# Feed-forward part of layer 0 woven into the attention loop, its gated value made by two products of VectorE from PSUM

## What is computed

```
x = x + tanh(g_xattn[0]) * causal attention(layernorm(x), ctx)        16 heads of 8
x = x + tanh(g_ffn[0])   * down(silu(gate(q(n))) * up(q(n)))          n = layernorm(x)
x = x + tanh(g_xattn[1]) * attention(layernorm(x), 8 chosen keys per head)
x = x + tanh(g_ffn[1])   * mixture of 16 experts, two chosen, and a shared one
```

## Time and profile before

| | us |
|---|---|
| median of 3 runs | 180.67 (180.66 to 180.68) |
| the profiled execution | 180.67 |
| its span, first to last instruction | 178.9 |
| TensorE busy, share of the span | 165.0, 92% |
| VectorE busy | 126.0, 70% |
| ScalarE busy | 83.7, 47% |
| GpSimd busy | 54.7, 31% |

### The profile page before, as it was taken

One profiled execution on the slowest core, in us unless ns is written; L12 is line 12 of the kernel. 1 busy time (PEld: TensorE's weight loads), 2 busy tenths in 40 slices (PEclk: granted clock), 3 DMA queues, 4 the chain that ended last, 5 costly groups with the idle time before them and its releaser, 6 DMA issues.

```text
span 178.9 us, 3936 instructions
## 1 busy us (share of the span) xinstructions
PE 165.0 (92%) x1530; PEld 105.9 (59%) x1538; DVE 126.0 (70%) x341; ACT 83.7 (47%) x154; POOL 54.7 (31%) x91
## 2 busy tenths in 40 slices
PE   7998999999999998888597799999999998999993
PEld 5644546665455454466365676647577665666672
DVE  0579365779779879698988698659838494654453
ACT  2255775654664655768566951365230313212210
POOL 8635652267884723436023005200002000000000
PEclk9999999999999999999999999999999999999999
DMA  5986000000000000000000000000000000100001
GB/s 157 395 297 286 0 0 5 4 2 4 2 4 4 0 4 0 0 4 2 0 4 0 0 0 4 0 2 0 2 4 0 0 0 0 59 4 0 0 0 59
DMA packets 1890, 5.83 MB, mean 33 GB/s; under 512 B 208, under 2 KB 592, under 8 KB 1744
## 3 DMA queue, kind: packets, MB, share of 16 engines
q1 hardware_dynamic: 1152, 4.01, 6.2%
q10 hardware_dynamic: 720, 1.57, 2.4%
HBM read 5.06 MB, written 0.52 MB: 31 GB/s over the span
## 4 chain that ended last, share of the span: by engine, by line
PE 68%; DVE 16%; ACT 7%; POOL 4%; issue 3%; POOLq 0%; DVEq 0%
PE banks L1342 10%; PE banks L1367 10%; PE banks L1345 10%; PE banks L1132 8%; DVE banks L748 4%; PE banks L1124 3%; PE banks L1178 3%; PE banks L1181 2%; POOL vz L264 2%; ACT ffn_work L536 2%; PE banks L1355 2%; ACT f_hqT L542 2%; PE banks L1162 2%; PE banks L1036 2%; PE banks L1152 2%
## 5 line engine op out<-in xcount | busy, mean ns | idle before, releaser
L748 DVE TENSOR_REDUCE banks<-banks 128x8 f32<-128x1024 f32 x16 | 19.7, 1230 | 10.8 <-PE banks L1132 10.8
L302 POOL TENSOR_SCALAR_AFFINE_SELECT pT<-pT 128x512 f32<-128x512 f32 x32 | 19.9, 644 | 24.2 <-ACT pT L459 24.1
L1367 PEld LDWEIGHTS banks<-ews,rest 128*128 128x128 f32 x160 | 20.6, 191 | 7.8 <-issue 7.7
L1036 PE MATMUL banks<-idle 128*128 128x256 bf16 x158 | 23.0, 293 | 1.2 <-DVE idle L659 1.2
L636 ACT ACTIVATE full<-banks 128x512 f32<-128x512 f32 x20 | 11.9, 593 | 21.9 <-PE banks L1342 21.9
L459 ACT ACTIVATE pT<-banks 128x512 f32<-128x512 f32 x32 | 17.3, 594 | 8.7 <-PE banks L1162 8.6
L1367 PE MATMUL banks<-ews,rest 128*128 128x128 f32 x160 | 21.0, 275 | 0.0
L1342 PE MATMUL banks<-nT,ews 128*128 128x512 f32 x40 | 20.6, 597 | 0.2
L994 DVE TENSOR_TENSOR xnT<-full,banks 128x512 f32<-128x512 f32 x20 | 13.7, 683 | 9.6 <-PE banks L1345 7.3
L1345 PE MATMUL banks<-nT,ews 128*128 128x512 f32 x40 | 20.4, 592 | 0.0
L1036 PEld LDWEIGHTS banks<-idle 128*128 128x128 bf16 x158 | 16.4, 105 | 5.2 <-DVE idle L659 1.2
(11 more groups left out here) (170 smaller groups left out, 287.7 us busy)
## 6 DMA issues: line engine op xcount, KB each, us to landing
ews<-in_ew SPq DMA_DIRECT2D x1, 1928.5 KB, 7.3
fws<-in_fw SPq DMA_DIRECT2D x1, 768.0 KB, 8.1
cT<-in_ctxT ACTq DMA_DIRECT2D x2, 256.0 KB, 5.3
x_all<-in_x SPq DMA_DIRECT2D x2, 256.0 KB, 4.7
lws<-in_lw ACTq DMA_DIRECT2D x1, 449.0 KB, 8.4
sels<-in_sel ACTq DMA_DIRECT2D x1, 320.0 KB, 8.7
a<-in_aw ACTq DMA_DIRECT2D x1, 256.0 KB, 5.1
out_x<-x_all SPq DMA_DIRECT2D x1, 256.0 KB, 2.0
```

Source lines behind the costliest of these rows:

```text
L302: nc.gpsimd.affine_select(out=probs, in_=probs, compare_op=ALU.is_ge, fill=0.0, base=0, pattern=[[0, HG], [1, S]], channel_multiplier=-1). ...
L748: V.tensor_reduce(bank[2 * p][:, 0:2 * HG], banks[p][:, :].rearrange("p (h k) -> p h k", h=2 * HG), AX.X, ALU.max).then_inc(sm["a_mx"], 1)
L1036: mm(bank[t][:, 0:2 * S], idle[:, 0:128], idle[:, :], start=True, stop=True)
L1367: last = mm(bank[t][:, b * D:(b + 1) * D], e_h[:, u, b * S:(b + 1) * S], expert(c)[2], start=(c == 0 and (b == 0 or s == 1 and b == 2)), s ...
```

## The change

Each sequence's FFN is done on its own, three to four iterations behind its attention, inside the loop. `x_prepare(m)` on GpSimd normalizes one sequence, `x_steps(m)` on VectorE finds its scale, `x_dequant(m)` on GpSimd makes the two factors, `x_scaled` and `xqT_copy` on ScalarE round it around `xq_transpose` (now float32). `gate_up(m)` always writes bank 5 (gate) and bank 4 (up). The gated value is silu(g) = g (1 + tanh(g/2)) / 2: ScalarE makes tanh into `f_sil` (`gate_tanh`), and `hidden(m)` on VectorE makes (tanh + 1) times gate from bank 5 into `f_p`, and that times up from bank 4 into `f_h`. Bank 4 also holds `xq_transpose`, `h_transposes` and `down` of all sequences, in turn. Within the loop come `gate_up` of sequences 0 to 4 and `down` of 0 to 2; `down(3)` and what belongs to sequences 5, 6, 7 follow it. The tail after the loop weaves these with layer 1's attention for sequences 0 to 3, in a new order. Weight rounding, the value copies and `v_proj(1)` move to earlier iterations, half of GpSimd's `own_tokens` to others. Normalizing sequences 4 to 7 for layer 1 moves to GpSimd. The two table loads around `exp3(0)` and the one behind the loop become one, before `hT_copy(7)`. Bodies that are not shown below keep their work (`h_transposes`, `down`: other bank; `hidden_steps`: L848 to L858; `ffn_residual`: with the statistics; `layer_stats`: with the aggregation of its one sequence).

```diff
+            def x_prepare(m):
+                pool.wait_ge(sm["q_mv"], m + 1)
...
+                nc.gpsimd.tensor_tensor(rstd[:, m:m + 1], ve[:, m:m + 1], mhalf[:, m:m + 1],
+                                        ALU.pow).then_inc(sm["q_rstd"], 1)
...
+                nc.gpsimd.tensor_scalar(tok(f_xn, m), tok(x_all, m), mv[:, 2 * m:2 * m + 1], rstd[:, m:m + 1],
+                                        ALU.subtract, ALU.mult).then_inc(sm["q_xn"], 1)
+            def x_dequant(m):
+                pool.wait_ge(sm["q_step"], XSTEPS * m + 2)
+                pool.wait_ge(sm["w_clip"], 1)
+                nc.gpsimd.tensor_scalar(f_deq[:, 0, m:m + 1], f_a[:, 1, m:m + 1], fclip[:, 0:1], 0.5,
+                                        ALU.mult, ALU.mult).then_inc(sm["q_deq"], 1)
...
                 causal(n, 2)
                 causal(n, 3)
...
+                if n >= 1:
+                    x_prepare(n - 1)
+                if n >= 1:
+                    x_dequant(n - 1)
...
+                elif n == 1:
                     spread_values(1)
+                elif n == 2:
+                    own_tokens(0, 0)
                 elif n == 3:
+                    own_tokens(1, 0)
+                elif n == 4:
                     own_tokens(0, 1)
-                elif n == 4:
+                elif n == 5:
                     own_tokens(1, 1)
...
+            bias_into_x(0)
+            x_prepare(7)
+            x_dequant(7)
+            rstd_of(2, 0)
+            rstd_of(1, 1)
+            pool.wait_ge(sm["ln_rstd1"], 2)
...
+            last.then_inc(sm["n3r"], 1)
+            bias_into_x(1)
+            rstd_of(2, 1)
...
+            def gate_tanh(m):
+                act.wait_ge(sm["f_gp"], m + 1)
+                act.wait_ge(sm["q_deq"], 2 * m + 2)
+                if m >= 2:
+                    act.wait_ge(sm["f_pr"], m - 1)
+                nc.scalar.activation(f_sil[:, u, :], bank[5][:, :], ACT.Tanh,
+                                     scale=f_deq[:, 0, m:m + 1]).then_inc(sm["f_th"], 1)
...
+            for n in range(B):
+                if n:
+                    exp(n - 1, 2)
+                    exp(n - 1, 3)
+                    if n >= 3:
+                        gate_tanh(n - 3)
+                    max_copy(n, 0)
+                if n == 1:
+                    xT_copy(1)
+                    weights_scaled(0)
+                elif n == 2:
+                    weights_out(0)
+                    weights_scaled(1)
+                elif n >= 4:
+                    hidden_scale(n - 4)
+                    if n == 4:
+                        weights_out(2)
+                exp(n, 0)
+                exp(n, 1)
+                if n >= 4:
+                    hT_copy(n - 4)
+                max_copy(n, 1)
+                if n == 0:
+                    k_copy(1)
+                    weights_abs(1)
+                    weights_abs(2)
+                elif n == 1:
+                    q_copy(1)
+                    v_copy(1)
+                    half1_masked(0)
+                elif n == 2:
+                    layer1_copy(0)
+                    weights_out(1)
+                    half1_masked(1)
+                    layer1_copy(1)
+                elif n == 3:
+                    half1_masked(2)
+                    half1_masked(3)
+                if n >= 2:
+                    x_scaled(n - 2)
+                    xqT_copy(n - 2)
+                if n == 3:
+                    weights_scaled(2)
+            exp(B - 1, 2)
+            exp(B - 1, 3)
+            gate_tanh(5)
+            hidden_scale(4)
+            hT_copy(4)
             kq_copy(0)
+            vo_copy(0)
+            x_scaled(6)
+            xT3_copy(0)
+            xqT_copy(6)
+            gate_tanh(6)
+            hidden_scale(5)
+            exp3(0)
+            hT_copy(5)
+            x_scaled(7)
+            xqT_copy(7)
             kq_copy(1)
...
+            gate_tanh(7)
+            pT3_copy(0)
+            hidden_scale(6)
+            hT_copy(6)
             vo_copy(1)
-            hidden_scale(2)
...
+            hidden_scale(7)
             nc.scalar.activation(table[:, 0:1], tg[:, 0:1], ACT.Silu)
             hT_copy(7)
...
+            def hidden(m):
+                dve.wait_ge(sm["f_th"], m + 1)
+                V.scalar_tensor_tensor(f_p[:, u, :], f_sil[:, u, :], 1.0, bank[5][:, :],
+                                       ALU.add, ALU.mult).then_inc(sm["f_pr"], 1)
+                dve.wait_ge(sm["f_pr"], m + 1)
+                dve.wait_ge(sm["f_up"], m + 1)
+                if m >= 2:
+                    dve.wait_ge(sm["f_htr"], m - 1)
+                V.scalar_tensor_tensor(f_h[:, u, :], bank[4][:, :], f_deq[:, 1, m:m + 1], f_p[:, u, :],
+                                       ALU.mult, ALU.mult).then_inc(sm["f_hr"], 1)
...
-                    layer_stats(n - 2, (n - 2) // HALF)
-                if n == 2:
+                    layer_stats(n - 2)
+                if n == 1:
                     weight_scales()
-                elif n == 3:
-                    q_masked(1, 1)
-                    q_masked(1, 3)
-                elif n == 5:
-                    aggregate(1, 0)
-                    weights_clipped(0)
-                elif n == 6:
-                    weights_clipped(2)
+                elif n == 2:
+                    weights_clipped(1)
+                elif n >= 4:
+                    hidden_steps(n - 4)
+                    if n == 4:
+                        weights_clipped(2)
                 top(n, 1)
                 split_max(n, 1)
+                if n >= 3:
+                    hidden(n - 3)
                 if n:
                     heads_out(n - 1)
+                if n >= 2:
+                    x_steps(n - 2)
+                if n >= 4:
+                    ffn_residual(n - 4)
                 if n == 0:
...
+                elif n == 1:
+                    weights_clipped(0)
                 elif n == 2:
                     q_masked(1, 0)
+                    q_masked(1, 1)
                 elif n == 3:
                     q_masked(1, 2)
-                elif n == 5:
...
             dve.wait_ge(sm["ld_l"], 16)
+            residual(6)
+            layer_stats(6)
+            hidden_steps(4)
+            hidden(5)
+            layer1_normalize(1, n3, 0, "n3r")
+            heads_out(7)
+            x_steps(6)
+            ffn_residual(4)
+            residual(7)
+            layer_stats(7)
+            hidden_steps(5)
+            softmax3_args(0)
+            hidden(6)
+            x_steps(7)
+            ffn_residual(5)
+            softmax3_normalize(0)
+            hidden_steps(6)
+            hidden(7)
+            residual3(0)
+            ffn_residual(6)
+            hidden_steps(7)
+            layer1_normalize(2, n4, 0, "n4r")
+            ffn_residual(7)
             aggregate(1, 1)
...
+            def h_transposes(m):
+                u = m % 2
+                pe.wait_ge(sm["f_htr"], m + 1)
+                pe.wait_ge(sm["f_hr"], min(m + 2, B))
+                if m:
...
+            def xq_transpose(m):
+                pe.wait_ge(sm["q_xs"], m + 1)
+                if m:
+                    pe.wait_ge(sm["f_hr"], m)
+                else:
+                    pe.wait_ge(sm["proj_out"], J_RAW + 2)
+                if m >= 2:
+                    pe.wait_ge(sm["f_res"], m - 1)
+                nc.tensor.transpose(bank[4][:, 0:S], tok(f_t, m), ident).then_inc(sm["f_xqTp"], 1)
...
+            def gate_up(m):
+                pe.wait_ge(sm["f_xqTs"], m + 1)
+                if m == 0:
+                    pe.wait_ge(sm["w_q"], 2)
+                else:
+                    pe.wait_ge(sm["f_th"], m)
+                    pe.wait_ge(sm["f_hr"], m)
+                mm(bank[5][:, :], f_xqT[:, bass.ts(m, S)], fq[:, 0, :], start=True, stop=True).then_inc(sm["f_gp"], 1)
+                mm(bank[4][:, :], f_xqT[:, bass.ts(m, S)], fq[:, 1, :], start=True, stop=True).then_inc(sm["f_up"], 1)
...
             for n in range(1, B):
                 score_masks(n, 0)
+                if n >= 5:
+                    down(n - 5)
                 max_rows(n - 1, 1)
                 scores(n, 0)
                 transposed_scores(n - 1, 1)
                 if n >= 2:
                     y_proj(n - 2)
+                if n >= 3:
+                    xq_transpose(n - 3)
                 subtract_max(n - 1, 1)
+                if n >= 3:
+                    gate_up(n - 3)
                 heads(n - 1, 0)
                 if n == 1:
                     x_transposes(1)
+                    weight_sums()
                 elif n == 2:
...
-                    layer1_proj(1)
+                    layer1_proj(0)
                 score_masks(n, 1)
                 max_rows(n, 0)
                 scores(n, 1)
                 transposed_scores(n, 0)
                 subtract_max(n, 0)
+                if n >= 4:
+                    h_transposes(n - 4)
                 heads(n - 1, 1)
```

(71 more changed lines are left out.)

422 lines of the change are left out of this document (89 added, 333 removed).

## The result

The changed kernel takes **210.26 us** (median of four runs, 209.76 to 211.04) against 180.67 (180.66 to 180.68): a ratio of 1.164, 95% interval 1.161 to 1.168, or 29.6 us more. The prediction had the direction, but not the size: 197, range 186 to 206. The profiled execution took 209.76 with a span of 208.0, so its 1.8 us outside the span are as before.

A forecast was written before the change was run, and what follows sets the result against it. One bank was taken to put VectorE and TensorE in turns, each waiting for the other. Start 50.1, four periods 46.2 and tail 34.2 gave 130.5 against 114.03, +16.5 on 180.67: 197 us, range 186 to 206.

The forecast's parts named there:

- Total work nearly even, order decides: Whole kernel: VectorE's total stays within 4 us of 126, so the order of the lists decides, not the work.
- Step 1: Loop iteration starting at T with top(n,0): top(n,1) can start at T+4.4, VectorE waiting 0.8 us for it.
- Step 2: Loop iteration: top(n,1) and its split end at T+6.0, then hidden(n-3) takes 1.5 us, to T+7.5.
- Step 3: Loop: TensorE stands from about T+5 to T+7.5 for hidden(n-3) to free bank 4; transposes and heads done at T+9.1.
- Step 4: Loop: VectorE's heads_out(n-1) waits for the heads from T+7.5 to T+9.1, 1.6 us.
- Period 11.55: Attention loop: one iteration lasts 11.55 us, and four of them 46.2, from 50.1 to 96.3.
- Rival C: Loop and tail: TensorE's clock falls to 1.2 GHz and products double in time, total up to 220; chance 0.06.
- Rival D: Loop: GpSimd late every period for x_dequant and own_tokens, periods 12.3 to 12.8, total 200 to 202; chance 0.12.
- The start 6.6: Before the full loop iterations: top(4,0) starts at 50.1, 6.6 us later than before, with a range of 2 to 8.
- the tail 34.2: From the end of VectorE's loop to hidden_proj(0): a chain across engines sums to 34.2 us, range 27 to 38.
- Expert stage unchanged: From hidden_proj(0) to the end: the same length as before, 64.9 us.
- Table load: Tail, ScalarE before hT_copy(7): the load with its one-element activation takes 1.4 us.

The follow-up runs named there:

- experiment 4: Changed kernel with VectorE's two products of hidden(n-3) moved from behind split_max(n,1) to ahead of top(n,1): 190.80 us.
- experiment 3: Changed kernel with 20 products that nobody reads filling TensorE's stand ahead of h_transposes(n-4) in the loop: 205.38 us.
- experiment 2: Changed kernel with GpSimd's own_tokens issued behind causal(n,1) of the next iteration: 204.53 us by two runs, median of all four 206.45.
- experiment 8: Changed kernel with transposes and down of sequences 5, 6, 7 in banks 3, 2, 3 instead of bank 4: 208.54 us.
- experiment 16: Reordered woven kernel of 180.72 us with scores3_bias(1) moved out of the expert stage to behind down(7): 180.16 us, ratio 0.996 to 0.999.
- experiment 12: Changed kernel with hidden(n-3) early, own_tokens later, other tail banks, ScalarE's start steps moved and the tail's end reordered: 181.18 us.

## Why the prediction was wrong, point by point

- **Total work nearly even, order decides:** right. VectorE 128.8 against 126.0, and experiment 4 moves 19.5 us with the same instructions.
- **Step 1, `top(n,1)` at T+4.4 with a wait of 0.8:** T+5.3 and 1.78. The term left out, GpSimd's lateness, sits here: `heads(n,0)` 0.83 late.
- **Step 2, both products 1.5:** right (1.46).
- **Step 3, TensorE stands for `hidden(n-3)`:** right, in place and releaser; the stand was 2.95 against some 2.5, since TensorE came to it 0.16 us behind the start of `top(n,1)` and not 0.6. **This is the step that failed:** it sums TensorE's work behind the stand at the full clock, transposes and heads at 0.45 and 1.02. They took 1.0 and 1.9, as the engine came out of its stand at the lower level. With the masks behind them that is over 1.5 us a period. The second term that was missing is GpSimd's, which the prediction left out of the sum and kept in its range.
- **Step 4, VectorE waits 1.6 for the heads:** 3.12, the same exchange with step 3's excess.
- **Period 11.55, four of them 46.2:** 57.8. That is 11.6 of the 13.3 us between 197 and 210.26. By experiment 3 (loop 52.5, its first period still at a clock of 0.77) the clock is at least 5.3 of it, and by experiment 2 GpSimd 3.8 to 5.7, the two not independent. The first period was the longest, 15.8: at a mean clock of 0.69, `top(4,1)` started at T+7.2.
- **Rival C** was the right mechanism with the wrong odds, 0.06. It rested on a row of before with 71% busy and a full clock; there the idle time came in pieces of at most 0.92 us, here in one of 3 us, and the mean busy share didn't tell them apart. The length of the stand alone doesn't either, since the one of 3.01 us in the tail left the clock full; what does is not shown by these runs. The Trainium skill, "TensorE: Matmul & The Clock Gate", section "HAM oscillation — how this bites in real kernels", describes a loop whose wait in each iteration lowers the clock each time; in the loop this trace agrees (0.66 to 0.87 in each period). C also foresaw the tail slowing; only its first 7 us did (0.76 from 107.2 to 114), and from 115 on it ran at 1.00.
- **Rival D** was right that GpSimd is late, in three of the four periods (0.64, 0.84 and 0.83); taking `own_tokens` off alone is worth 3.8 to 5.7 us, at or above the 3 to 5 that it was priced at.
- **The start 6.6, the tail 34.2:** 5.9 and 34.4. The tail's sum hit, but experiment 8 shows that its bank waits are worth only 1.7, so that the sum hit is in part luck.
- **Expert stage unchanged:** wrong by 1.5. `scores3_bias(1)` (0.86) had been moved into it, and `w_transposes(0)` waited 0.51 for VectorE.
- **Table load:** 1.28 and 0.20 on the chain, 1.40 from the start of the load to that of `hT_copy(7)`, as taken (1.4). The Trainium skill, "ScalarE: Activation LUTs", section "What ACT_TABLE_LOAD costs", has 2.66 for a switch; this trace doesn't bear that out.

## What to carry to other kernels

Where two engines hand a bank to and fro, put the instruction that frees it into the wait that its engine already has; here that one line was worth 19.5 of 29.6 us. A stand of TensorE has to be priced twice, once for its length and once for what runs slower behind it; neither the busy share nor the length of one stand told here where the clock would fall, so keep a rival with the lower clock in the sum and look at the granted clock first. And before calling a stage unchanged, look for steps that the new order moved into it: in a stage where one engine never waits, each of them costs its full time.

## What the runs showed of the hardware

- Filling a stand with products that nobody reads made the period shorter, 12.5 for 13.8 us. But a stand of 3.01 us in the tail of the changed kernel left the clock at 1.00, and in experiment 16 the clock fell to 0.82 (79.6 to 89 us) though no stand from 48 us on was longer than 0.53 us.
- The lower clock can come after the stands, while TensorE is fully busy: 8.00 of 8 us busy at 0.79 in experiment 12. Where in the program it falls can change with a small edit elsewhere, and the time of a kernel near that edge scatters by 1 us (180.12 to 181.73 in experiment 16) where the kernel before keeps within 0.4.
- An elementwise step of VectorE on 68 columns with two inputs in SBUF took 1.27 us beside a two-input pass of GpSimd on 512 columns and 0.23 without it; the like step 0.5 us earlier ran beside GpSimd's one-input pass and took 0.23. The Trainium skill, "GPSIMD Engine Reference", section "1. Specifications", names the SBUF interface as shared with VectorE, with contention for VectorE's instructions that have two SBUF inputs. The trace agrees for the step that took 1.27; the step of 0.23 had two SBUF inputs as well and was not slowed.
- GpSimd's power on one column took 0.57 us, on four 1.04: four times the columns cost less than twice the time.
